# Barriers replaced by narrow waits, weight sums moved into the K/V phase, and PSUM emptying moved behind the next quantization, in an attention plus ternary FFN block on eight cores

## The chip, the cores and the metric

The kernel runs on all 8 NeuronCores of one Trainium2 chip. The cores do not exchange data: each computes 1024 of the 8192 rows of the output. The time is that of the slowest core, in device microseconds, as the median of several executions. The profile shows one execution on the slowest of its cores, here core 1.

## The reference, cut to what matters

```python
# x: (2, 4096, 2048). Weights: w_dq (1536,2048), w_uq (2048,1536), w_dkv (512,2048),
# w_ukv (4096,512), w_out (2048,2048), w_gate and w_up (8192,2048), w_down (2048,8192)
def weight_quant(w):                       # three values: -scale, 0, +scale
    scale = clip(mean(abs(w)), 1e-5)       # one mean over the whole matrix
    return clip(round(w / scale), -1, 1) * scale
def act_quant(x):                          # 8 bits, scale by the row's largest value
    s = 127 / clip(max(abs(x), axis=-1), 1e-5)
    return clip(round(x * s), -128, 127) / s
def bitlinear(x, w): return act_quant(x) @ weight_quant(w).T
def attn(x):                               # 16 heads of 128, causal
    q = x @ w_dq.T @ w_uq.T
    k, v = split(x @ w_dkv.T @ w_ukv.T)
    return softmax(q @ k.T / sqrt(128) + mask) @ v @ w_out.T
xn = layernorm(x)
y = x + attn(xn) + bitlinear(silu(bitlinear(xn, w_gate)) * bitlinear(xn, w_up), w_down)
```

The scales of the three large matrices need the sum of absolute values of each whole matrix before any of it can be quantized.

## The kernel before

The whole program is written out by one Python function, `emit`, once for each engine. Every wait is written by hand: `inc` counts an engine's own semaphore and waits for it, `wt(engine, semaphore, value)` waits, `dinc` counts a DMA by 16, and `barrier()` (L255) lets every engine wait for all others and for all DMAs so far. In the code T is TensorE (PE in the profile), V is VectorE (DVE), S is ScalarE (ACT), G is GpSimd (POOL), SY is SyncE (SP).

The stages of a core, with the times of core 1:

- P0a (0 to 744 us): layernorm of 4608 key rows in 36 tiles, transposes, and the 512-wide compressed keys and values `ckv`. P0b (to 920): the same for the core's 1024 own rows, with 8-bit quantization. P0c (to 1032): w_ukv loaded, the quantized rows transposed and stored.
- P0d (to 1165) and P0e (to 1340): the two query projections, weights streamed by `stream_blocks` (L509), 12 and 16 column blocks.
- Attention (to 3153): eight groups of two heads (loop at L670). In a group PE first makes K (18 banks of 128x512, L681, copied to `kg` by DVE, L687) and V (36 banks of 128x256, L693, copied to `vg`, L699) in four banks in turn, and then runs the sweep over 36 key tiles: scores (L602), exp on ACT (L609), row sums (L641), values (L645). The border between the core's two halves depends on the core, so the sweep stands in the program eight times, each under `If_eq` (L709), and a core skips seven of them: core c skips c before its own and 7 - c behind it.
- P1out (to 3325): output projection, L747, result to DRAM.
- P2a (3385 to 4660): gate and up for 16 chunks `hc` of 512 hidden columns. For a chunk, SP loads eight 1 MB blocks, DVE quantizes them (L833, L836 for gate into `tg`, L841, L844 for up into `tu`; two sets, by `hc % 2`), PE runs 128 gate matmuls into all eight banks (one bank for each row tile `tb`, L855), ACT applies silu into `hg` (L861), PE runs 128 up matmuls into the same banks (L871), and DVE multiplies each bank with `hg` into `hstg` (L880) and takes the maximum (L882); POOL stores `hstg` (L887). DVE's order is: quantize chunk hc, empty chunk hc, quantize chunk hc + 1. PE's first gate matmul of a chunk waits for all the emptying of the one before (`hv_prev`).
- P2b (to 4895): the hidden rows are read back (`hbuf`), quantized (L917 on ACT, L923 and L924 on DVE) and transposed (L932, L937), in four quarters for each of eight row tiles.
- P2c (to 5542): down projection, 16 output blocks `oc`. SP loads eight slabs of 512 KB in turn into two buffers, DVE quantizes them (L966, L968) into `tdq`, PE runs four quarters of 32 matmuls (L981) into one of two bank pairs, DVE copies the pair out (L987). DVE's order is: quantize oc, copy out oc, quantize oc + 1.
- P3: transposes back and the sum.

The sums of absolute values are made beside this by `pump_scale` (L373). It takes the next of 192 blocks of 1 MB, loads it (by POOL unless told otherwise) into one of one or two buffers, after the last sum on that buffer, and has it summed by ACT (`on_s=True`, L396) or DVE (L401). 36 blocks are summed on DVE in P0a; 8, 12 and 32 on ACT in P0c, P0d and P0e; 12 behind each of the eight sweeps on ACT (96); the last 8 on ACT behind P1out. Since PE's wait for the next group (`ms_sweeps`) is taken before them, the 12 sums run beside the K/V work of the next group. The calls behind a sweep are

```python
            ms_sweeps = cnt["mS"]
            for _ in range(6):
                pump_scale(1, (xt0,), on_s=True, dq=G, psem="p0")
                pump_scale(1, (xt1,), on_s=True, dq=SY, psem="c0")
```

Of the kernel before, what the change touches and what calls it, by code (L numbers as in the profile page):

```python
# [40 lines left out]
def build_nc():  # L41
# [184 lines left out]
    def emit(nc, ACTIVE, cnt):  # L226
# [443 lines left out]
        for g in range(NGRP):  # L670
# [3 lines left out]
            kv_ev = {}  # L674
            for kt in range(9):
                k0 = kt * 512
                for hh in range(HPG):
# [128 lines left out]
        hv_prev = 0  # L806
        for hc in range(FD):
# [5 lines left out]
            for q in range(4):  # L813
# [15 lines left out]
                if q == 0:  # L829
# [16 lines left out]
                    op0=ALU.is_gt, op1=ALU.subtract), V)  # L846
            tmg = [0] * NQT
            for q in range(4):
                wt(T, "mV", qg_q[q])
                if q == 0 and hc >= 1:  # L850
                    wt(T, "mV", hv_prev)
                for f4 in range(4):
                    fc = 4 * q + f4
# [22 lines left out]
            for tb in range(NQT):  # L876
                wt(V, "mT", tmu[tb])
                if hc >= 1 and tb == 0:
                    wt(V, "g2", hs_dg[hc - 1])
                inc(V.tensor_tensor(out=hstg[:, tb, :], in0=bank(tb), in1=hg[:, tb, :],  # L880
                                    op=ALU.mult), V)
                inc(V.reduce_max(out=hmaxa[:, hc, tb:tb + 1], in_=hstg[:, tb, :], axis=AX,  # L882
                                 apply_absolute_value=True), V)
            hv = cnt["mV"]
            hv_prev = hv
            wt(G, "mV", hv)
            gd = G.dma_start(out=hs_d.rearrange("(tb p) (hc c) -> tb p hc c", p=128, c=512)[:, :, hc, :].rearrange("tb p c -> p tb c"),  # L887
                             in_=hstg[:])
            hs_dg[hc] = dinc(gd, "g2")
# [242 lines left out]
```

How the kernel before makes its waits and increments, by code:

```python
        def then_inc(self, *a, **k):  # L196
            return self
# [1 line left out]
        def _wait_ge(self, *a, **k):  # L199
            return self
# [36 lines left out]
        def inc(instr, eng):  # L237
            s = e2s[id(eng)]
            cnt[s] += 1
            instr.then_inc(sems[s], 1)
            eng.wait_ge(sems[s], cnt[s])
            return cnt[s]
# [1 line left out]
        def dinc(instr, q):  # L244
            cnt[q] += 16
            instr.then_inc(sems[q], 16)
            return cnt[q]
# [1 line left out]
        def wt(eng, s, val):  # L249
            if val > 0:
                eng.wait_ge(sems[s], val)
# [3 lines left out]
        def barrier():  # L255
            for nm, _e in ENGS:
                cnt[nm] += 1
            me = EP.__getattribute__(
                {"tensor": T, "vector": V, "scalar": S, "gpsimd": G, "sync": SY}[ACTIVE],
                "_r") if False else None
            ap = {"tensor": T, "vector": V, "scalar": S, "gpsimd": G, "sync": SY}[ACTIVE]
            ap.nop().then_inc(sems["m" + {"tensor": "T", "vector": "V", "scalar": "S",
                                          "gpsimd": "G", "sync": "Y"}[ACTIVE]], 1)
            for nm, _e in ENGS:
                if nm != "m" + {"tensor": "T", "vector": "V", "scalar": "S",
                                "gpsimd": "G", "sync": "Y"}[ACTIVE]:
                    ap.wait_ge(sems[nm], cnt[nm])
            for dq in DMA_SEMS:
                if cnt[dq]:
                    ap.wait_ge(sems[dq], cnt[dq])
```

## Time and profile before

| | us |
|---|---|
| median of three runs | 5635.7 |
| lowest, highest | 5617.92, 5694.85 |
| the profiled execution | 5667.2 |
| its span on core 1, the slowest | 5665.4 |
| spans of cores 0, 2, 3 | 5649.4, 5622.2, 5647.3 |
| spans of cores 4, 5, 6, 7 | 5616.2, 5567.3, 5638.2, 5581.2 |

A row of the groups by line gives line, engine, operation, the tiles written and read, their shapes, the count, then busy time and mean of one, and last the idle time of that engine just before these instructions with what ended it. "issue" means that the profile shows nothing that the engine waited for. The chain of work that ended last is followed back from the end. Durations of matmuls are modelled: one takes about 0.38 us in the table even where the next starts 0.22 us behind it, so rates are read from start times.

### The profile page before, as it was taken

The numbers are of one execution on the slowest core, as the hardware profiler recorded it, in microseconds if no ns is written. First come the engines' busy times: TensorE is split into PE (matmuls) and PEld (weight loads), VectorE is DVE, ScalarE is ACT, GpSimd is POOL, SyncE is SP. The second block draws the span as 40 slices with busy tenths as digits, with TensorE's granted clock in tenths as the row PEclk, the third lists the DMA queues.
The fourth block names the chain that finished last, engine by engine and source line by source line (L and its number), as shares of the span: only waits on it lengthen the run. The fifth ranks groups of instructions, "written<-read, shape, count | busy, mean of one in ns | idle before, by whom it ended". The sixth has DMA issues, their size and how long they took to land.

```text
span 5665.4 us, 45000 instructions; the slowest of 8 cores (5567.3 to 5665.4 us)
## 1 busy us (share of the span) xinstructions
PE 3325.9 (59%) x13124; PEld 1231.6 (22%) x13124; DVE 2107.6 (37%) x2998; ACT 1099.9 (19%) x1101; POOL 129.8 (2%) x197
## 2 busy tenths in 40 slices
PE   2443422566565645645645447777787763588883
PEld 1111110222111111111111213333333321233332
DVE  3444434222122231221222124555445536644444
ACT  3333332222323223223233110000000002100000
POOL 0000000000000000000000000000000000000000
PEclk9655655788677776877778879988998885698775
DMA  4223213774012022021120554554344424333334
GB/s 145 104 104 119 97 52 104 210 235 127 31 61 91 1 91 71 21 92 32 60 91 17 159 176 127 149 148 119 119 134 149 149 95 149 109 109 112 97 104 148
DMA packets 344785, 610.04 MB, mean 108 GB/s; under 512 B 10530, under 2 KB 228130, under 8 KB 306978
## 3 DMA queue, kind: packets, MB, share of 16 engines
q1 hardware_dynamic: 310546, 399.08, 22.8%
q0 software_dynamic: 33808, 205.53, 11.3%
q8 instruction: 232, 3.80, 0.3%
q14 instruction: 199, 1.63, 0.1%
HBM read 554.24 MB, written 50.33 MB: 107 GB/s over the span
## 4 chain that ended last, share of the span: by engine, by line
PE 44%; DVE 20%; issue 14%; DMA 13%; ACT 8%; DVEq 1%; ACTq 0%; SPq 0%; POOL 0%; POOLq 0%; PEldq 0%
PE psp L981 7%; PE psp L602 4%; PE psb L871 4%; PE psb L641 3%; PE psp L871 3%; PE psb L645 3%; PE psp L693 3%; PE psp L681 3%; DMA xt<-wdT 2%; DVE tgq L836 2%; DMA gsq<-wgT 2%; ACT xntb L340 2%; DVE hstg L880 2%; DMA dslab<-wdT 2%; DMA pe<-wuT 2%
## 5 line engine op out<-in xcount | busy, mean ns | idle before, releaser
L981 PE MATMUL psp<-hqfm,tdq 128*128 128x512 bf16 x2048 | 528.0, 424 | 118.8 <-DVE tdq L968 108.1
L855 PE MATMUL psb<-tgq,xqfm 128*128 128x512 bf16 x1024 | 292.8, 399 | 238.3 <-DVE tgq L836 231.1
L609 ACT ACTIVATE ptile<-psp 128x1024 bf16<-128x1024 f32 x288 | 294.8, 1024 | 573.8 <-PE psp L602 572.0
L357 PE MATMUL psp<-identb,xntb 128*128 128x128 bf16 x352 | 93.3, 265 | 485.7 <-ACT xntb L340 286.1
L681 PE MATMUL psp<-ckv,wukv 128*128 128x512 bf16 x576 | 162.1, 407 | 331.4 <-issue 261.1
L981 PEld LDWEIGHTS psp<-hqfm,tdq 128*128 128x128 bf16 x2048 | 213.0, 106 | 433.4 <-issue 323.3
L629 DVE TENSOR_TENSOR ptile<-ptile,masksb 128x512 bf16<-128x512 bf16 x64 | 27.2, 425 | 738.8 <-ACT ptile L609 738.8
L855 PE MATMUL psp<-tgq,xqfm 128*128 128x512 bf16 x1024 | 287.7, 398 | 9.5
L871 PE MATMUL psb<-tuq,xqfm 128*128 128x512 bf16 x1024 | 272.9, 379 | 27.4 <-ACT hg L861 13.8
L602 PE MATMUL psp<-qfm,kg 128*128 128x512 bf16 x576 | 222.2, 475 | 109.9 <-PE psb L645 66.5
L871 PE MATMUL psp<-tuq,xqfm 128*128 128x512 bf16 x1024 | 270.7, 379 | 9.7
L641 PE MATMUL psb<-ptile,onesb 128*64 128x512 bf16 x576 | 215.3, 462 | 94.9 <-PE psp L602 66.7
L861 ACT ACTIVATE hg<-psb,sgs 128x512 f32<-128x512 f32 x64 | 44.0, 687 | 1130.6 <-PE psb L855 1123.5
L880 DVE TENSOR_TENSOR hstg<-psb,hg 128x512 f32<-128x512 f32 x64 | 44.3, 692 | 537.9 <-PE psb L871 528.8
L687 DVE CAST kg<-psp 128x512 bf16<-128x512 f32 x144 | 99.6, 692 | 387.9 <-PE psp L681 387.9
L396 ACT ACTIVATE xt<-xt 128x2048 f32<-128x2048 f32 x96 | 183.3, 1909 | 213.4 <-DMA xt<-wdT 122.7
L645 PE MATMUL psb<-ptile,vg 128*128 128x512 bf16 x576 | 217.9, 468 | 0.0
L693 PE MATMUL psp<-wukv,ckv 128*128 128x256 bf16 x1152 | 171.9, 271 | 74.7 <-PE psp L693 72.4
L855 PEld LDWEIGHTS psb<-tgq,xqfm 128*128 128x128 bf16 x1024 | 100.6, 101 | 386.2 <-issue 288.6
L968 DVE SCALAR_TENSOR_TENSOR tdq<-dslab,thr,dcma 128x1024 bf16<-128x1024 f32 x128 | 164.4, 1285 | 14.1 <-DVE dcma L966 0.9
L699 DVE CAST vg<-psp 128x256 bf16<-128x256 f32 x288 | 122.4, 425 | 122.1 <-PE psp L693 122.0
L362 DVE CAST xnf<-psp 128x128 bf16<-128x128 f32 x352 | 102.6, 292 | 174.8 <-PE psp L357 167.9
(157 smaller groups left out, 3963.8 us busy)
## 6 DMA issues: line engine op xcount, KB each, us to landing
gsq<-wgT SPq DMA_DIRECT2D x64, 1024.0 KB, 11.3
usq<-wuT SPq DMA_DIRECT2D x64, 1024.0 KB, 10.9
dslab<-wdT SPq DMA_DIRECT2D x128, 512.0 KB, 4.1
pa<-wgT POOLq DMA_DIRECT2D x36, 1024.0 KB, 5.0
xt<-xk SPq DMA_DIRECT2D x36, 1024.0 KB, 4.9
hs<-hstg POOLq DMA_DIRECT2D x16, 2048.0 KB, 12.0
hbuf<-hs SPq DMA_DIRECT2D x32, 1024.0 KB, 5.4
xt<-wdT POOLq DMA_DIRECT2D x28, 1024.0 KB, 5.8
```

The lines of the kernel that those rows point to most:

```text
L396: sm = inc(S.activation(out=sbuf[:], in_=sbuf[:], func=AF.Abs, accum_out=accTw[:, mi, col:col + 1]), S)
L602: mm = T.matmul(out=bank(sp + hh), lhsT=kg[:, hh, (j - jlo) * 128:(j - jlo + 1) * 128], rhs=qfm[:, h0 + hh, qc0:qc0 + 512], start=True, st ...
L609: a = S.activation(out=ptile[:, pb, :, :].rearrange("p h c -> p (h c)"), in_=bank2(sp), func=AF.Exp, scale=SCALE, bias=EXPB)
L641: T.matmul(out=(psb6 if hh == 0 else psb7)[0:64, :], lhsT=onesb[:, 0:64], rhs=ptile[:, pb, hh, :], start=st, stop=sp_)
L645: mm = T.matmul(out=bank(hh), lhsT=vg[:, j - jlo, hh * 128:(hh + 1) * 128], rhs=ptile[:, pb, hh, :], start=st, stop=sp_)
L681: mm = T.matmul(out=bank(b), lhsT=wukv[:, cc, (h0 + hh) * 128:(h0 + hh + 1) * 128], rhs=ckv[:, cc, k0:k0 + 512], start=(cc == 0), stop=(cc ...
L693: mm = T.matmul(out=bank(b)[:, 0:HPG * 128], lhsT=ckv[:, cc, jj * 128:(jj + 1) * 128], rhs=wukv[:, cc, 2048 + h0 * 128:2048 + (h0 + HPG) * ...
L855: mm = T.matmul(out=bank(tb), lhsT=xqfm[:, fc, tb * 128:(tb + 1) * 128], rhs=tg[:, fc, :], start=(fc == 0), stop=(fc == FD - 1))
L871: mm = T.matmul(out=bank(tb), lhsT=xqfm[:, fc, tb * 128:(tb + 1) * 128], rhs=tu[:, fc, :], start=(fc == 0), stop=(fc == FD - 1))
L880: inc(V.tensor_tensor(out=hstg[:, tb, :], in0=bank(tb), in1=hg[:, tb, :], op=ALU.mult), V)
L968: e_done[ei % 2] = inc(V.scalar_tensor_tensor(out=fq, in0=fl, scalar=thr[:, 4:5], in1=fa, op0=ALU.is_gt, op1=ALU.subtract), V)
L981: mm = T.matmul(out=bank(bp + nh), lhsT=tdq[:, hcc, :], rhs=hqfm[:, hcc, nh * 512:(nh + 1) * 512], start=(hcc == 0), stop=(hcc == 63))
```

## The change

- P0d, P0e and the first group: two barriers go. POOL waits for PE's last P0d matmul, and in front of the first group POOL, DVE and PE wait for the ends of P0e on ACT and DVE; the first four banks carry waits for their last copies.
- The sums behind the sweeps go. In the K/V phase of each group DVE calls `pump_scale(1)` after every fourth copy, up to the 52nd of 54: 13 sums in a group, on DVE, with buffers `xt0` and `xt1`, both loaded by POOL. With the 88 before, that is all 192. `pump_scale` also waits for the last sum that used the same semaphore.
- P2a: DVE quantizes chunk hc + 1 before it empties chunk hc, and PE's first matmul into a bank waits for the product (L880) of that bank only.
- P2a to P2b: the barrier and SP's wait for all stores go. SP waits for the last quantization and, quarter by quarter, for the store that it reads. `cmp_a` moves out of `hbuf`'s place.
- P2b to P2c: the barrier goes; SP and DVE wait for ACT's last instruction.
- P2c: DVE quantizes block oc + 1 before it copies out block oc; PE waits for the copy two blocks back by the bank pair.
- P2c to P3: the barrier goes; POOL and SP wait for PE, PE for DVE.

```diff
-    cmp_a = AT("cmp_a", [128, FD, 512], BF16, offset=SB0 + 168 * KB)
+    cmp_a = AT("cmp_a", [128, 4, 512], BF16, offset=SB0 + 200 * KB)
...
+                lastp = sc_done.get(ps)
+                if lastp and lastp != prev:
+                    wt(dq, lastp[0], lastp[1])
...
             pump_scale(1, (pd0,), on_s=True)
-        barrier()
+        wt(G, "mT", cnt["mT"])
...
             pump_scale(2, (pe0, pe1), on_s=True)
-        barrier()
+        p0e_T = cnt["mT"]
+        p0e_V = cnt["mV"]
+        p0e_S = cnt["mS"]
...
-            kv_ev = {}
+            if g == 0:
+                kv_ev = {2: ev_bank.get(2, 0), 3: ev_bank.get(3, 0),
+                         4: tb_ev[4], 5: tb_ev[5]}
+                wt(G, "mS", p0e_S)
+                wt(G, "mV", p0e_V)
+                wt(V, "mS", p0e_S)
+                wt(T, "mV", p0e_V)
+            else:
+                kv_ev = {}
+            evi = 0
...
                     kv_ev[b] = inc(ev, V)
+                    evi += 1
+                    if evi % 4 == 0:
+                        pump_scale(1)
...
                 kv_ev[b] = inc(ev, V)
+                evi += 1
+                if evi % 4 == 0 and evi <= 52:
+                    pump_scale(1)
...
             ms_sweeps = cnt["mS"]
-            for _ in range(6):
-                pump_scale(1, (xt0,), on_s=True, dq=G, psem="p0")
-                pump_scale(1, (xt1,), on_s=True, dq=SY, psem="c0")
...
+            if pend is not None:
+                ehc, etmu = pend
+                for tb in range(NQT):
+                    wt(V, "mT", etmu[tb])
+                    if ehc >= 1 and tb == 0:
+                        wt(V, "g2", hs_dg[ehc - 1])
+                    inc(V.tensor_tensor(out=hstg[:, tb, :], in0=bank(tb), in1=hg[:, tb, :],
+                                        op=ALU.mult), V)
+                    ev_tb[tb] = cnt["mV"]
+                    inc(V.reduce_max(out=hmaxa[:, ehc, tb:tb + 1], in_=hstg[:, tb, :], axis=AX,
+                                     apply_absolute_value=True), V)
+                wt(G, "mV", cnt["mV"])
...
-                if q == 0 and hc >= 1:
-                    wt(T, "mV", hv_prev)
...
+                        if fc == 0 and hc >= 1:
+                            wt(T, "mV", ev_tb[tb])
...
-        wt(SY, "g2", cnt["g2"])
-        barrier()
...
+        for vv in sorted(sq_done.values()):
+            wt(SY, "mV", vv)
...
+                if tb == 0:
+                    wt(SY, "g2", hs_dg[4 * qt + 3])
...
-        barrier()
+        p2b_V = cnt["mV"]
+        p2b_S = cnt["mS"]
...
+        wt(SY, "mS", p2b_S)
+        wt(V, "mS", p2b_S)
+        ev_bank[4] = p2b_V
...
+            if pend_c is not None:
+                eoc, ebp, etm = pend_c
+                wt(V, "mT", etm)
+                ev = V.tensor_copy(out=ffnb[:, eoc, :], in_=bank2(ebp))
+                ev_bank[ebp] = inc(ev, V)
...
-            tm = tmq_prev[3]
-            wt(V, "mT", tm)
-            ev = V.tensor_copy(out=ffnb[:, oc, :], in_=bank2(bp))
-            ev_bank[bp] = inc(ev, V)
-        barrier()
+            pend_c = (oc, bp, tmq_prev[3])
...
+        wt(G, "mT", cnt["mT"])
         ao_dd = dinc(G.dma_start(out=aofm[:], in_=aos_d.rearrange("f p c -> p f c")), "g2")
+        wt(SY, "mT", cnt["mT"])
         wt(T, "g2", ao_dd)
+        wt(T, "mV", cnt["mV"])
```

## Rows read from the trace of the kernel before

**Rows 1.** The page of core 1: busy times, and the chain by engine.
```profile
PE 3325.9 (59%) x13124; PEld 1231.6 (22%) x13124; DVE 2107.6 (37%) x2998; ACT 1099.9 (19%) x1101; POOL 129.8 (2%) x197
PE 44%; DVE 20%; issue 14%; DMA 13%; ACT 8%; DVEq 1%; ACTq 0%; SPq 0%; POOL 0%; POOLq 0%; PEldq 0%
```
**Rows 2.** Groups by line, forms apart; busy, mean ns | idle before, releasers.
```profile
L981 PE MATMUL psp<-hqfm,tdq 128*128 128x512 bf16 x2048 | 528.0, 424 | 118.8 <-DVE tdq L968 108.1 <-PE psp L981 10.2 <-DVE dcma L966 0.5
L855 PE MATMUL psb<-tgq,xqfm 128*128 128x512 bf16 x1024 | 292.8, 399 | 238.3 <-DVE tgq L836 231.1
L681 PE MATMUL psp<-ckv,wukv 128*128 128x512 bf16 x576 | 162.1, 407 | 331.4 <-issue 261.1 <-ACT xt L396 37.1 <-PE psp L681 29.8
```
**Rows 3.** Timeline of P2a: start, us, engine, line [idle before]; 15 such PE borders.
```profile
3610.30 0.69 DVE L880 TENSOR_TENSOR hstg<-psb,hg 128x512 f32<-128x512 f32 x1 [32.14 <-PE psb L871]
3611.95 0.69 DVE L880 TENSOR_TENSOR hstg<-psb,hg 128x512 f32<-128x512 f32 x1 [0.17 <-DVE hmaxa L882]
...
3623.61 1.29 DVE L833 TENSOR_SCALAR cmp_a<-gsq,thr 128x2048 bf16<-128x2048 f32 x1 [0.25 <-DVE hmaxa L882]
3625.00 2.35 DVE L836 SCALAR_TENSOR_TENSOR tgq<-gsq,thr,cmp_a 128x2048 bf16<-128x2048 f32 x1
...
3627.60 1.01 PE L855 MATMUL psb<-tgq,xqfm 128*128 128x512 bf16 x2 [13.80 <-DVE tgq L836]
```
**Rows 4.** Timeline of P2c, end of a pass and start of the next.
```profile
5005.42 7.07 PE L981 MATMUL psp<-hqfm,tdq 128*128 128x512 bf16 x32 [0.26 <-PE psp L981]
...
5018.77 9.30 PE L981 MATMUL psp<-hqfm,tdq 128*128 128x512 bf16 x32 [6.29 <-DVE tdq L968]
```
**Rows 5.** Timeline of K and V copies on DVE, second group.
```profile
1594.92 0.69 DVE L687 CAST kg<-psp 128x512 bf16<-128x512 f32 x1 [0.58 <-PE psp L681]
...
1600.88 0.42 DVE L699 CAST vg<-psp 128x256 bf16<-128x256 f32 x1 [0.43 <-PE psp L693]
```
**Rows 6.** Timeline of PE at three gaps: of core 1, of core 7, of core 4.
```profile
1339.41 1.01 PE L681 MATMUL psp<-ckv,wukv 128*128 128x512 bf16 x2 [22.66 <-issue]
...
1850.48 2.17 PE L602 MATMUL psp<-qfm,kg 128*128 128x512 bf16 x4 [33.98 <-issue]
...
1790.37 6.46 PE L681 MATMUL psp<-ckv,wukv 128*128 128x512 bf16 x16 [15.81 <-issue]
```
**Rows 7.** Groups by line again: the sums on DVE, ACT's table loads before the sweeps.
```profile
L401 DVE TENSOR_REDUCE accTw<-pa 128x1 f32<-128x2048 f32 x36 | 82.3, 2286 | 6.2 <-DVE xnf L362 4.6 <-DVE ckv L437 1.5
L609 ACT ACT_TABLE_LOAD x8 | 10.3, 1283 | 401.7 <-PE psp L602 401.7
```
**Rows 8.** DMA issues: queue, count, KB each, median us to landing.
```profile
xt<-wdT POOLq DMA_DIRECT2D x28, 1024.0 KB, 5.8
pe<-wgT POOLq DMA_DIRECT2D x8, 1024.0 KB, 9.3
aofm<-aos POOLq DMA_DIRECT2D x1, 4096.0 KB, 18.2
```
**Rows 9.** The chain in order of time (start, us): attention's end, P1out's, P2a's, P2b's.
```profile
3102.18 1.28 ACT L396
...
3328.32 15.74 DMA pt<-wdT
...
4646.81 12.06 DMA hs<-hstg
4660.57 9.34 DMA hbuf<-hs
...
4896.74 4.15 DMA dslab<-wdT
```
**Rows 10.** Windows of V, P2a, P2c: us, five engines' busy, granted clock, DMA, GB/s.
```profile
1364.00:1395.00 31.00, 21.49 (x144) 11.49 (x144) 15.75 (x37) 0.00 (x0) 0.00 (x0) 1.00 0.00 1
...
3950.00:4010.00 60.00, 54.44 (x239) 22.82 (x236) 23.34 (x17) 5.50 (x8) 0.00 (x0) 1.00 0.47 140
...
5211.00:5245.00 34.00, 31.54 (x119) 12.35 (x116) 11.45 (x12) 0.00 (x0) 0.00 (x0) 0.81 0.33 93
```

More of the change, by code:

```diff
@@ L397, in pump_scale @@
                                           accum_out=accTw[:, mi, col:col + 1]), S)
-                    sc_done[id(sbuf)] = ("mS", sm)
+                    sc_done[id(sbuf)] = sc_done[ps] = ("mS", sm)
                 else:
@@ L402, in pump_scale @@
                                           apply_absolute_value=True), V)
-                    sc_done[id(sbuf)] = ("mV", vm)
+                    sc_done[id(sbuf)] = sc_done[ps] = ("mV", vm)
         xn_sm = [0] * (NKC + NQT)
@@ L805, in emit @@
         silu_sm = [0] * NQT
-        hv_prev = 0
+        ev_tb = [0] * NQT
+        pend = None
         for hc in range(FD):
@@ L846, in emit @@
                     op0=ALU.is_gt, op1=ALU.subtract), V)
+            if pend is not None:
[10 more added lines that the diff above has]
+                wt(G, "mV", cnt["mV"])
+                gd = G.dma_start(out=hs_d.rearrange("(tb p) (hc c) -> tb p hc c", p=128, c=512)[:, :, ehc, :].rearrange("tb p c -> p tb c"),
+                                 in_=hstg[:])
+                hs_dg[ehc] = dinc(gd, "g2")
             tmg = [0] * NQT
@@ L875, in emit @@
             tq_used[setq] = cnt["mT"]
[L876 to L889, printed above, removed]
-        wt(SY, "g2", cnt["g2"])
-        barrier()
+            pend = (hc, list(tmu))
+        ehc, etmu = pend
+        for tb in range(NQT):
+            wt(V, "mT", etmu[tb])
+            if tb == 0:
+                wt(V, "g2", hs_dg[ehc - 1])
+            inc(V.tensor_tensor(out=hstg[:, tb, :], in0=bank(tb), in1=hg[:, tb, :],
+                                op=ALU.mult), V)
+            inc(V.reduce_max(out=hmaxa[:, ehc, tb:tb + 1], in_=hstg[:, tb, :], axis=AX,
+                             apply_absolute_value=True), V)
+        wt(G, "mV", cnt["mV"])
+        gd = G.dma_start(out=hs_d.rearrange("(tb p) (hc c) -> tb p hc c", p=128, c=512)[:, :, ehc, :].rearrange("tb p c -> p tb c"),
+                         in_=hstg[:])
+        hs_dg[ehc] = dinc(gd, "g2")
+        for b_ in (4, 5, 6, 7):
+            tb_ev[b_] = cnt["mV"]
         maybe_stop('P2a')
@@ L897, in emit @@
         QS = ("w0", "w1", "x0", "x1")
+        for vv in sorted(sq_done.values()):
+            wt(SY, "mV", vv)
         for tb in range(NQT):
             for qt in range(4):
+                if tb == 0:
+                    wt(SY, "g2", hs_dg[4 * qt + 3])
                 if tb >= 1:
@@ L944, in emit @@
                             scalar2=None, op0=ALU.mult), V)
-        barrier()
+        p2b_V = cnt["mV"]
+        p2b_S = cnt["mS"]
         maybe_stop('P2b')
         dsrc = wd_d.rearrange("(hc p) (oc c) -> hc p oc c", p=128, c=128)
+        wt(SY, "mS", p2b_S)
+        wt(V, "mS", p2b_S)
+        ev_bank[4] = p2b_V
         tmq_prev = [0, 0, 0, 0]
         e_done = {0: 0, 1: 0}
+        pend_c = None
         for oc in range(FD):
@@ L984, in emit @@
                 tmq_prev[qt] = inc(mm, T)
-            tm = tmq_prev[3]
-            wt(V, "mT", tm)
-            ev = V.tensor_copy(out=ffnb[:, oc, :], in_=bank2(bp))
-            ev_bank[bp] = inc(ev, V)
-        barrier()
+            pend_c = (oc, bp, tmq_prev[3])
+        eoc, ebp, etm = pend_c
+        wt(V, "mT", etm)
+        ev = V.tensor_copy(out=ffnb[:, eoc, :], in_=bank2(ebp))
+        ev_bank[ebp] = inc(ev, V)
         maybe_stop('P2c')
+        wt(G, "mT", cnt["mT"])
         ao_dd = dinc(G.dma_start(out=aofm[:], in_=aos_d.rearrange("f p c -> p f c")), "g2")
+        wt(SY, "mT", cnt["mT"])
         wt(T, "g2", ao_dd)
+        wt(T, "mV", cnt["mV"])
         y_ev = [0] * NQT
```

## The prediction

> **What bounds the kernel now.** I read five views in this order. First the page: engine busy times, then the chain of work that ended last [rows 1]. TensorE is busy in 59% of 5665.4 us, DVE in 37%. The chain is 44% PE, 20% DVE, 14% issue, 13% DMA: no engine is full, and the kernel is a row of stages with joins. Then the groups by line, for what ended PE's idle time [rows 2]. The large entries are 238.3 us before the gate matmuls (L855), nearly all ended by DVE's quantizing (L836), 118.8 us before the down matmuls (L981), ended by L968, and 331.4 us before the first K matmuls of the head groups (L681), "issue". Last the timeline and the chain at each join, and the windows for the clock.
>
> What the reader is to see. **Gate/up stage:** PE stops 13.80 us at a chunk border (the one before 3627.60; there are 15), because DVE empties eight banks first and only then quantizes the next weights [rows 3]. **Down stage:** PE ends a pass at 5012.5, DVE copies it out and quantizes two slabs, PE starts again at 5018.77 after 6.29 us and its first 32 matmuls take 9.30 us instead of 7.07. A pass is four quarters of 7.07 + 0.26 = 29.3 us and the border adds 6.03 + 2.23 = 8.3: 37.6 us [rows 4]. **Attention:** K and V of a head pair are made at 1.28 and 0.85 us a bank with DVE 0.69 and 0.42 us busy in each [rows 5], at clock 1.00 [rows 10]. The abs-sum of a weight block runs on ACT beside it, off the path. PE then idles about 39 us between sweep and next pair while it skips six branches.
>
> **The change part by part, on core 1 of the profiled run.** The sum is made against its own 5665.4 us.
>
> (a) P0d, P0e, attention lose two barriers. In P0e the abs-sum loads set the end: PE was idle 22.66 us before 1339.41 [rows 6], and the new DVE wait on ACT's last sum keeps that. P0e's first abs-sum loads start 2 us earlier and the first four K banks are already filled: -6. Bounds 0 and -14.
>
> (b) The abs-sums go to DVE inside K/V: 13 per group. Each is L401's 2.286 us [rows 7]. V phase: four copies at 0.42 plus 0.15 between plus the sum is 4.6 us against PE's 4 x 0.85 = 3.4; nine times +1.2 = 11. K phase: four copies and the sum 5.7 against 5.1; four times +0.6 = 2.4. With the waits of PE for a bank and of DVE for PE behind each sum (0.1 to 0.2) I take 15.3. DMA: each of two buffers is needed again two sums later, 9.4 us in the V phase and 11.4 in the K phase; the sum takes 2.3, the way to the issue 0.6, the landing 5.8 us at the median for such a load, 9.3 for the first ones of P0e beside other weights [rows 8]. I take 6.7, near the first because nothing else loads; it just fits: +16 per group, 8 x 16 = +128. Bounds: +122 (never waited for) and +216 (landing 9.3 us: a pair takes 12.5 us, in the V phase 5.7 more than PE's 6.8, 4.5 x 5.7 + 1.5 = +27 per group). What is queued behind a late landing is every following K/V copy, and PE with it after four banks.
>
> (c) No abs-sum loads while PE skips branches. Core 7 skips seven before its sweep with no loads beside it in 33.98 us, 4.9 each; core 1's six behind its sweep, with the loads running, are the 261.1 and 37.1 us of L681 in [rows 2] less the first 22.66: 39.4 at each of seven borders [rows 6]. At 5 us each six take 30: -9 x 7 = -63. Bounds: 0 (the difference is of the code, not the traffic) and -71. The Trainium skill (Runtime: NRT & Kernel Launch, Instruction fetch mechanics) says that a taken branch out of the fetched pages must get its target by DMA. By that rule the loads and the skips share the DMA engines and the sum keeps its -63; by a count of instructions alone it would be 0.
>
> (d) ACT keeps the Exp table: the 1.28 us load stands on the chain before each sweep, and now only before the first [rows 7]: 7 x 1.28 = -9.
>
> (e) Behind the last sweep ACT worked at its table and sums from 3102.18 [rows 9] to 3153, with the barrier behind them. PE ends the sweep about then, so its skips (30 us) end it now at 3133: -20. On core 6, which skips one branch, it is 51 - 7 = -44.
>
> (f) 8 x 13 = 104 sums instead of 96 leave none of the eight whose loads ran from 3328.32 on [rows 9], to 3379. The 6 MB for the next stage are loaded there anyway; 4 MB took 18.2 us [rows 8], so I take 24: -27. Bounds -33 (18.2) and -20.
>
> (g) P2a. DVE's chunk border order is turned: quantize next, then empty. Quantizing is 8 x (1.29 + 2.35 + 0.27) = 31 us, emptying 8 x 1.65 = 13 [rows 3]; 44 of about 70 us, so DVE is done about 20 us before PE. At the border PE's fc = 0 matmul of each bank now waits for that bank only. The first emptying starts 3.5 us before PE's last matmul ends (3610.30 against 3613.8), the eighth product ends 7 x 1.65 + 0.70 - 3.5 = 8.8 later; PE itself needs 1.7 for eight, so it loses 7.4 instead of 13.8: 15 x 6.4 = 96. Of the 231.1 us that ended on L836, the 24 beyond 15 x 13.8 lie inside the chunks and go too: -120. Bounds -144 (borders at 5.8 us) and -33 (all eight products and maxima needed, 13.2).
>
> (h) P2a to P2b. The 12.06 us store and 9.34 us load [rows 9] lie behind work: three of the four loads are early, and the first three quarters (32 of them in 4670 to 4895, 7.0 each) cover the fourth: -21 (bounds -9, the store still waited for, and -22). P2b to P2c: 4.15 us slab load [rows 9] and barrier: -7. SP's moved waits hold only loads that come later.
>
> (i) P2c. With the slabs of the next pass quantized in this one, PE has four quarters of 7.32 us, 29.3 instead of 37.6 [rows 4]. The 6.29 us stop holds a copy (about 1.2) and two slabs, so DVE needs some 2.4 a slab, 4.8 a quarter, and a slab buffer turns round in 4.15 [rows 9] + 2.4 = 6.5; both under 7.3. 15 x 8.3 = -124. P2c took 636 us from its first matmul, 43 more than 15 x 37.6 + 29.3: in its later part the clock read 0.81 [rows 10], a quarter then 7.07 / 0.81 = 8.7. A pass of 36 instead of 29.3 costs 6.5, so the stretch was 7 passes of 43, some 300 us; if it keeps its length it covers 8.5 shorter ones, 55: +12 to +15. Net -109. The last join: -2.
>
> Sum: -6 +128 -63 -9 -20 -27 -120 -21 -7 -109 -2 = -256, so 5409 on core 1. Core 6 (span 5638.2) has no such gap, so (c) is 0 and (e) -44: -217, 5421. It is the slowest then. The profiled execution was 5667.2 us, 31.5 above the median of three, so the forecast is 5423 - 31.5, rounded to 5395.
>
> **Rivals.**
> R1, late landings in (b): at 9.3 us 8 x 11 = +88, 5483. For it: two loads on POOL's one queue; against: nothing else loads then.
> R2, the skips stay as long: core 1 becomes 5472, 5442 at the median. Core 7's 33.98 speaks against it; for it, core 4 skipped three in 15.81 us with loads running, 5.3 each [rows 6].
> R3, a denser PE is granted less. In P2c it was 0.81 at PE 31.5 of 34 us busy [rows 10]. At 8.7 against 7.07 us per 32, all 4096 matmuls of P2a cost +209 and the rest of P2c +45: 5649, no change. Against: P2a held 1.00 with PE 54.4 of 60 us busy [rows 10]. The Trainium skill (TensorE: Matmul & The Clock Gate, Seeing it yourself) says that a die with three cores in dense matmuls goes to 13/16 clock and stays there while the load lasts; by that rule R3 would be the case, and this trace, where P2a is at 1.00 with eight cores at work, does not agree.
> R4, PE half idle in K/V falls to 1.2 GHz (0.50): K banks take 2.0 us, 18 x 0.55 x 8 = +80, 5475. Against: 1.00 in the V phase with PE 21.5 of 31 us busy [rows 10].
> R5, slower than before: the landings in (b) decide alone. Beyond 7 us each us costs some 6 us per group, 48 in all; the gain is 240 us, so at 12 us all is lost, and at 13 the time is about 5670. The longest of [rows 8] is 9.3.
> R6, the change doesn't reach the path: the new waits (DVE on ACT at P0e, DVE's emptying at the borders) stop as long as the barriers. P2a -33 instead of -120 gives 5482.
>
> **How the numbers follow.** Forecast 0.55 (own range 5340 to 5450); R1 0.11, R2 0.12, R3 0.08, R4 0.06, R5 0.03, R6 0.05. A change of 2% (5523 and 5748) is what a measurement can tell. Faster: all but R3 and R5, and 0.03 of misses within the others, 0.86. Same 0.11. Slower 0.03. Range 5320 to 5500: it takes in R1, R2, R4, R6 and leaves out R3, R5 and the forecast's tails, 0.2.
>
> **What would show it.** (b) K/V of a group 72 us instead of 56, DVE idle for "DMA xt" under 3 us a group. (c) L681's idle about 30 us on core 1. (d) one Exp table load. (g) borders of 7 to 8 us. (i) no gap between passes, 29.3 us each, or about 36 at 0.81. Wrong if K/V goes past 80 us, if P2a reads 0.81, or if the skips stay at 39.

## The result, and the profile after

Ten runs of each kernel: 5466.8 us median for the changed one (5422.4 to 5486.3), 5665.6 for the one before (5617.9 to 5694.9). The ratio is 0.964, with a 95% interval of 0.960 to 0.969: **faster, by 199 us**. The forecast was 5395 us, in a range of 5320 to 5500. It was tied to the first three runs of before, whose median was 5635.7; against that the forecast gain was 241 us. In some executions of any kernel one die is over 1% longer at a lower granted clock: medians here are of all executions, ratios, intervals and figures core by core of the others.

The profiled execution took 5486.2 us, 5484.7 on its slowest core, again core 1. First its page: busy times and the chain by engine.

```profile
PE 3483.7 (64%) x13124; PEld 1267.1 (23%) x13124; DVE 2345.4 (43%) x3102; ACT 882.8 (16%) x886; POOL 154.4 (3%) x245
PE 52%; DVE 19%; issue 15%; DMA 7%; ACT 6%; DVEq 1%; PEldq 1%; SPq 0%; ACTq 0%; POOL 0%; POOLq 0%
```

PE's share of the chain rose from 44 to 52% and DMA's fell from 13 to 7 [rows 1]. PE's busy time rose too, by 158 us, with the same 13124 matmuls: somewhere they run slower. The groups by line, forms apart, say where (busy, mean ns of one | idle before, releasers).

```profile
L1028 PE MATMUL psp<-hqfm,tdq 128*128 128x512 bf16 x2048 | 454.4, 380 | 25.2 <-PE psp L1028 17.4 <-DVE tdq L1010 6.8 <-DVE dcma L1008 0.8
L888 PE MATMUL psb<-tgq,xqfm 128*128 128x512 bf16 x1024 | 310.8, 421 | 53.3 <-DVE hstg L871 33.9 <-DVE tgq L854 8.1 <-PE psb L904 4.1
L710 PE MATMUL psp<-wukv,ckv 128*128 128x256 bf16 x1152 | 289.2, 404 | 102.2 <-PE psp L710 68.7 <-DVE kg L701 30.4 <-DVE vg L716 3.1
L695 PE MATMUL psp<-ckv,wukv 128*128 128x512 bf16 x576 | 163.2, 409 | 268.0 <-issue 207.1 <-DVE kg L701 32.5 <-PE psp L695 22.4
L404 DVE TENSOR_REDUCE accTw<-xt 128x1 f32<-128x2048 f32 x104 | 237.7, 2286 | 21.2 <-DVE vg L716 13.1 <-DVE kg L701 5.1 <-DMA xt<-wuT 2.5
L614 ACT ACT_TABLE_LOAD x8 | 10.3, 1283 | 945.9 <-PE psp L607 945.9
```

Against [rows 2]: the wait of the down matmuls (now L1028) fell from 118.8 to 25.2 us, of one half of the gate matmuls (L888) from 238.3 to 53.3, of the K matmuls (L695) from 331.4 to 268.0. But the V matmuls (L710) take 404 ns in the mean; before they took 271. The sums on DVE (L404) are 2286 ns each as forecast and waited 2.5 us in all for a landing. ACT still loads the Exp table eight times, not once.

The stages of core 1, from the first and last matmul of each line in the timelines, in us. "Low" is the 1.2 GHz level, granted clock 0.50.

| | before | after | change | forecast |
|---|---|---|---|---|
| start to the end of the first K/V | 1394.3 | 1407.6 | +13 | +10 |
| K/V of the seven other groups | 7 x 55.2 | 7 x 73.6 | +129 | +112 |
| from V to the first scores, 8 | 39.3 | 36.8 | -2 | 0 |
| sweeps with the table loads, 8 (time at low clock) | 875.5 (479) | 897.5 (541) | +22 | -9 |
| last scores to next K, 7 | 391.4 | 324.4 | -67 | -63 |
| last scores to output projection | 75.9 | 56.1 | -20 | -20 |
| output projection | 162.9 | 189.4 | +26 | 0 |
| to the gate/up stage | 64.5 | 34.6 | -30 | -27 |
| gate/up stage | 1245.3 | 1178.2 | -67 | -120 |
| to the down stage | 270.6 | 246.0 | -25 | -28 |
| down stage | 634.8 | 472.5 | -162 | -109 |
| to the end | 124.5 | 126.5 | +2 | -2 |
| sum | | | -181 | -256 |

The three large differences from the forecast in the last stages (output projection, gate/up and down stage) have one part in common: a stretch at granted clock 0.81. Windows of core 1 in the output projection, late gate/up and the whole down stage show it (us, busy times of five engines, clock, DMA):

```profile
3237.00:3427.00 190.00, 148.07 (x512) 55.19 (x512) 40.10 (x47) 0.00 (x0) 14.67 (x15) 0.78 0.38 102
4100.00:4240.00 140.00, 126.65 (x439) 48.05 (x437) 78.94 (x64) 5.50 (x8) 2.34 (x2) 0.75 0.42 137
4886.00:5358.00 472.00, 453.58 (x2047) 196.14 (x2046) 275.11 (x267) 0.00 (x0) 0.00 (x0) 1.00 0.50 140
```

The down stage, at 0.81 for 262 us before, now had 1.00 throughout; the output projection had 137 us at 0.81 (+26) and gate/up 265 us: four of its periods took 80.4 to 81.6 us, where others took 71.7. On core 4, which saw 0.81 in neither stage in either run, gate/up went from 1237.0 to 1141.5 (-96), the down stage from 592.3 to 472.5 (-120), the output projection stayed at 164. Those are the gains of the change in these stages.

### The profile page after: what moved, and what is told of

It reads as the page before. It is cut to its first block, busy times and chain, and to the rows that moved or that the text cites. A ratio compares the mean times of both kernels' runs of the same rounds, so it can differ in the third digit from the quotient of the medians.

```text
span 5484.7 us, 44659 instructions; the slowest of 8 cores (5351.4 to 5484.7 us)
## 1 busy us (share of the span) xinstructions
PE 3483.7 (64%) x13124; PEld 1267.1 (23%) x13124; DVE 2345.4 (43%) x3102; ACT 882.8 (16%) x886; POOL 154.4 (3%) x245
## 4 chain that ended last, share of the span: by engine, by line
PE 52%; DVE 19%; issue 15%; DMA 7%; ACT 6%; DVEq 1%; PEldq 1%; SPq 0%; ACTq 0%; POOL 0%; POOLq 0%
PE psp L1028 6%; PE psp L710 4%; PE psb L888 4%; PE psp L888 4%; PE psp L607 4%; PE psb L904 4%; PE psb L646 4%; PE psp L904 4%; PE psb L650 4%; DVE accTw L404 3%; ACT xntb L340 2%; DVE hqfm L974 2%; DMA pe<-wuT 2%; PE psb L435 2%; DMA dslab<-wdT 1%
## 5 line engine op out<-in xcount | busy, mean ns | idle before, releaser
L1028 PE MATMUL psp<-hqfm,tdq 128*128 128x512 bf16 x2048 | 454.4, 380 | 25.2 <-PE psp L1028 17.4
L710 PE MATMUL psp<-wukv,ckv 128*128 128x256 bf16 x1152 | 289.2, 404 | 102.2 <-PE psp L710 68.7
L888 PE MATMUL psp<-tgq,xqfm 128*128 128x512 bf16 x1024 | 314.2, 419 | 58.8 <-DVE hstg L871 49.2
L888 PE MATMUL psb<-tgq,xqfm 128*128 128x512 bf16 x1024 | 310.8, 421 | 53.3 <-DVE hstg L871 33.9
L695 PE MATMUL psp<-ckv,wukv 128*128 128x512 bf16 x576 | 163.2, 409 | 268.0 <-issue 207.1
L904 PE MATMUL psb<-tuq,xqfm 128*128 128x512 bf16 x1024 | 286.2, 394 | 25.2 <-ACT hg L894 13.9
L904 PE MATMUL psp<-tuq,xqfm 128*128 128x512 bf16 x1024 | 284.2, 394 | 10.5 <-ACT hg L894 0.9
L1028 PEld LDWEIGHTS psp<-hqfm,tdq 128*128 128x128 bf16 x2048 | 196.3, 98 | 283.0 <-issue 57.5
L404 DVE TENSOR_REDUCE accTw<-xt 128x1 f32<-128x2048 f32 x104 | 237.7, 2286 | 21.2 <-DVE vg L716 13.1
L710 PEld LDWEIGHTS psp<-wukv,ckv 128*128 128x128 bf16 x1152 | 123.8, 125 | 267.7 <-issue 231.4
L1008 DVE TENSOR_SCALAR dcma<-dslab,thr 128x1024 bf16<-128x1024 f32 x128 | 96.4, 753 | 158.5 <-PE psp L1028 104.6
```

Source lines behind the costliest of these rows:

```text
L695: mm = T.matmul(out=bank(b), lhsT=wukv[:, cc, (h0 + hh) * 128:(h0 + hh + 1) * 128], rhs=ckv[:, cc, k0:k0 + 512], start=(cc == 0), stop=(cc ...
L710: mm = T.matmul(out=bank(b)[:, 0:HPG * 128], lhsT=ckv[:, cc, jj * 128:(jj + 1) * 128], rhs=wukv[:, cc, 2048 + h0 * 128:2048 + (h0 + HPG) * ...
L1028: mm = T.matmul(out=bank(bp + nh), lhsT=tdq[:, hcc, :], rhs=hqfm[:, hcc, nh * 512:(nh + 1) * 512], start=(hcc == 0), stop=(hcc == 63))
```

## Experiments

Twelve kernels ran. Stage times below are of core 1 of the profiled execution, unless another core is named.

### e1 and e2: the change in two halves

```diff
+            for _ in range(6):
+                pump_scale(1, (xt0,), on_s=True, dq=G, psem="p0")
+                pump_scale(1, (xt1,), on_s=True, dq=SY, psem="c0")
```

e1 is the changed kernel with the sums taken out of K/V and put back behind the sweeps as above. e2 is the kernel before with the attention part alone.

> The changed kernel with its 96 sums put back behind the sweeps on ACT, two DMA queues, the rest of the change kept. On core 1 the two profiles give for the attention part: first K banks -28 us, K/V of the first group +41, of the seven others +18.4 each, gaps between last scores and next K -9.6 each (55.9 to 46.3), end of the last sweep to the output projection -20, output projection to gate/up -30: together +20. Theory A (the sums in K/V cost more than the shorter skips give back): K/V 55 us, gaps 56, and about 20 us faster than the changed kernel, some 220 under the kernel before. Theory B (the attention part is a gain, and what looks like its cost is the scatter of the clock): 20 us slower than the changed kernel, 180 under the kernel before.

> The kernel before with the attention part of the change alone (two early barriers, sums on DVE in K/V); gate/up and down stages and their barriers as before. Theory A: +20 us against the kernel before, no difference that counts. Theory B: 20 us or more faster. Prediction on record: its terms for this part come to +3. K/V of a group 73 us, gap 46 on core 1.

e1: 5421.5 us median of four (5376.6 to 5458.1), no interval; the kernel before beside it 5650.0. e2: 5694.6, ratio 1.0063, interval 1.0024 to 1.0103. In e1 K/V is back to 55.5 us and the gap to 54.5; gate/up 1137, down 473. In e2 K/V is 73.3, the gap 45.2; gate/up 1238, down 594. Four executions are too few to tell 20 us; e11 is e1 again, beside the changed kernel itself (e12).

> The changed kernel with the sums back behind the sweeps, beside the changed kernel on the same chip, to tell 20 to 30 us. Theory A: 5420 to 5450 us, 20 to 40 under the changed kernel. Theory B: not under it.

> The changed kernel itself, for the comparison with the sums behind the sweeps: 5450 to 5490 us, ratio 0.964 to the kernel before by every theory.

e11: 5373.4, ratio to the kernel before beside both 0.9538 (0.9481 to 0.9595). e12: 5444.4, ratio 0.9659 (0.9613 to 0.9704). **Theory A holds, B falls:** alone, the attention part makes the kernel slower by 0.2 to 1.0%, and the changed kernel with the sums back behind the sweeps is faster by 71 us. The whole gain is in the two feed-forward stages and their joins. The 71 are more than the 20 to 40 expected, and a part of that is which core counts. Core by core (medians of six each) e12 is longer by 39, 60, 41, 91, 81, 80, 70 and 101 us on cores 0 to 7: little where many branches are skipped behind the sweep, most on core 7, which skips none there. On core 1, from which the expectation came, it is 60 and not 20 to 40; the rest is open. On core 4, the slowest of e12, three skip there: K/V costs the same 129 us (7 x 73.6 against 7 x 55.2), the gaps give back 26 (7 x 31.2 against 7 x 34.9). The same holds in e2: core 7 is 112 us longer than in the kernel before, core 2, the slowest there, only 15, and the time is that of the slowest core. So e2's 0.6% understates what the sums in K/V cost.

### e3 and e4: the same sums on ACT, held back or free

```diff
                     if evi % 4 == 0:
-                        pump_scale(1)
+                        wt(S, "mV", kv_ev[b])
+                        pump_scale(1, on_s=True)
```

This is e3, in both loops; e4 has the second added line without the wait.

> The changed kernel with the 13 sums of a group on ACT, each started by the same K/V copy behind which DVE's stood; loads on POOL's queue as before. Theory A (DVE's 2.29 us sums in a row with the copies are the whole price): K/V back to 55 us from 73, PE at clock 1.00 in it, gaps stay at 46 on core 1, 147 us less than the changed kernel less up to 5 us a group where ACT ends late: 100 to 147 us faster than it. Theory C (the loads beside K/V slow its copies or matmuls): K/V stays above 65. Theory D (the low clock of PE in the V phase is set by something other than its stalls): V phase stays at 45 us at clock 0.50.

> The same 13 sums on ACT with no wait for a copy: ACT starts them when the sweep ends, so that their loads run while PE skips branches, as in the kernel before. Theory A1 (the loads lengthen the skips): gap on core 1 back from 46 to 56, K/V 55, so 7 x 10 = 70 us slower than the gated version on core 1, nothing on core 7, which skips nothing behind its sweep. Theory A2 (the skips became shorter by the code between them): gap stays at 46 and this kernel is as fast as the gated one.

e3: 5355.9 us, ratio 0.945 (0.930 to 0.960, from three executions, classed as unclear). It is 294 us under its kernel before, where the changed one is 199 under: 95 more, near the 100 to 147 of Theory A. e4: 5378.7 us, no interval. The V phase of the fourth group as a window, of the changed kernel and then of e3:

```profile
2071.00:2116.00 45.00, 35.84 (x143) 15.48 (x144) 34.69 (x44) 0.00 (x0) 4.33 (x9) 0.50 0.61 202
```
```profile
2015.00:2045.00 30.00, 20.89 (x140) 11.19 (x140) 15.17 (x36) 14.28 (x16) 4.23 (x8) 1.00 0.70 242
```

45 us at clock 0.50 against 30 at 1.00, with more traffic beside it in e3 (242 against 202 GB/s). So theories C and D fall: the loads don't hold K/V up, nor is the clock low without DVE's sums; DVE's sums do both. K/V of all groups of e3 is 24.9 + 30.4 us. ACT ends its last sums late, by some 2 us a group: core 1 stands 51 us in front of its eight sweeps instead of 37.

The gap is the test of the skips. PE's rows for the first K matmuls of a group, three of e3 and then three of e4:

```profile
1990.79 4.84 PE L695 MATMUL psp<-ckv,wukv 128*128 128x512 bf16 x12 [28.86 <-issue]
2209.61 5.83 PE L695 MATMUL psp<-ckv,wukv 128*128 128x512 bf16 x16 [28.27 <-issue]
2428.35 7.07 PE L695 MATMUL psp<-ckv,wukv 128*128 128x512 bf16 x16 [28.24 <-issue]
```
```profile
1998.89 1.44 PE L695 MATMUL psp<-ckv,wukv 128*128 128x512 bf16 x3 [36.62 <-issue]
2220.53 1.86 PE L695 MATMUL psp<-ckv,wukv 128*128 128x512 bf16 x4 [38.49 <-issue]
2450.54 5.81 PE L695 MATMUL psp<-ckv,wukv 128*128 128x512 bf16 x16 [34.72 <-issue]
```

The two programs differ by 13 waits of ACT in a group. With the loads held back six skips take 28.5 us in these rows, with the loads running 36.6; over all seven gaps the means are 28.3 and 38.0. Means of the whole gap: 45.0 against 54.7 on core 1; on core 7, which skips nothing behind its sweep, 18.2 against 18.1. **The loads lengthen the skips (A1)**, as step (c) had it. ACT's sums run there too in e4; they were not separated from their loads. But the DMA queues of one such gap point at the loads. First e3 (1961 to 1991 us), then e4 (1961 to 1999): queue and kind, packets, MB, share of 16 engines.

```profile
q8 instruction: 11, 0.18, 3.9%
```
```profile
q0 software_dynamic: 1034, 7.55, 56.4%
q8 instruction: 11, 0.18, 2.4%
```

In each of the seven gaps of either run the same 11 instruction packets of 16 KB land on q8, about two for each skipped branch; in e4 they come further apart, beside 7.55 MB of loads. The Trainium skill (Runtime: NRT & Kernel Launch, Instruction fetch mechanics) says that a taken branch's target is fetched by DMA when it lies outside the fetched pages; these two runs agree, at 4.7 us a skip without and 6.3 with the loads.

### e5, e9 and e10: why the clock is low in the V phase

```diff
-                b = 2 + (jj % 4)
+                b = 2 + ((jj + 2) % 4)
```

This is e5. e9 cuts each sum in two, `sbuf[:, 0:D // 2]` and `sbuf[:, D // 2:D]`, one behind every second copy. e10 is both.

> The changed kernel, only the order of banks in the V phase turned by two, so that the first V bank is the one copied longest ago and PE doesn't stand 3.6 us behind the copies of the last two K banks. Theory E (that stop lets the clock fall, and at 1.2 GHz a V bank takes 1.27 us, so PE bounds the V phase): clock 1.00 in the V phase, which goes from 45.0 to the 41 us that DVE needs (9 x 4.6), K/V from 73.4 to about 66. Theory F (the clock falls because PE has a third of idle time as long as DVE sets the pace): clock still 0.50, V phase 45, K/V about 70 to 73.

> The changed kernel with each sum of 128x2048 cut into two of 128x1024 and one placed after every second copy; the first half is overwritten by the second, so the scales leave half of each block out. DVE's work in the V phase is nearly the same (4 copies and two halves, about 4.8 us for four banks), its longest stop of the copies falls from 2.3 to 1.2 us. Theory J (long stops of PE pull the clock down in the V phase): clock 1.00 there, V phase about 43 us. Theory F (any pace of DVE that leaves PE a share of idle time does, however it is cut): clock 0.50, V phase 45 to 47 us.

> The kernel with halved sums and, in addition, the V banks turned by two (half of each block is left out of the scales again). Each of the two edits alone left a stop of PE at the K to V step, 2.1 us with turned banks and 3.7 to 4.1 us with halved sums, and in both the clock fell at that stop. Here DVE's pace is the same and the longest stop is about 1 us. Theory K (a stop at the step lets the clock fall, and then PE at 1.2 GHz is kept low by its own slow pace): clock 1.00 through most of the V phase, which takes the 42 to 43 us that DVE needs. Theory F (DVE's pace alone lets it fall): 0.50 within the first quarter of the phase, V phase 44 to 46 us.

The V phases as windows, e5 and then e9:

```profile
2023.00:2069.00 46.00, 35.23 (x144) 15.20 (x142) 37.90 (x46) 0.00 (x0) 4.75 (x9) 0.53 0.60 209
```
```profile
2078.00:2122.00 44.00, 34.88 (x140) 14.86 (x139) 35.69 (x53) 0.00 (x0) 4.76 (x9) 0.50 0.55 192
```

The clock stayed low in all three; K/V took 71, 73 and 72 us. But none took the stop away as meant. It moved two banks on (e5, 1.90 us idle), stayed in front of V (e9, 4.00) or moved and shrank to 1.7 us in most groups (e10), and on core 1 the clock fell around that stop each time, 2 us behind it at the latest. So E, J and K are not refuted by these. What speaks for F is the rare case of a clock that came back within the phase. PE in e9, last group of core 1, some banks of it:

```profile
3005.67 1.01 PE L743 MATMUL psp<-wukv,ckv 128*128 128x256 bf16 x4 [0.26 <-PE psp L743]
3006.94 0.60 PE L743 MATMUL psp<-wukv,ckv 128*128 128x256 bf16 x4 [0.26 <-PE psp L743]
...
3012.47 0.60 PE L743 MATMUL psp<-wukv,ckv 128*128 128x256 bf16 x4 [0.64 <-DVE vg L749]
...
3015.05 0.60 PE L743 MATMUL psp<-wukv,ckv 128*128 128x256 bf16 x4 [1.13 <-DVE vg L749]
```

Banks come 1.27 us apart up to 3006.94 and 0.85 apart behind it: clock 1.00. PE then waits for DVE, never longer than 1.13 us, and at 3016.8 the clock is 0.50 again. e10 shows the same in one group of core 1 (1.00 from 2314.8 to 2325.0), and in e6, with whole sums, the clock came back in the sixth group and fell again behind stops of 1.34 and 2.06 us. So waits of about 1 us, as DVE's pace makes them, are enough for a fall; in the other groups the stop at the step may be what starts it.

At 0.50 a V bank takes PE 1.27 us, 36 of them 45.7. What DVE needs is seen in its rows: two sums of the changed kernel, then two of e5, both at clock 0.50.

```profile
2079.13 2.29 DVE L404 TENSOR_REDUCE accTw<-xt 128x1 f32<-128x2048 f32 x1 [0.17 <-DVE vg L716]
2084.19 2.29 DVE L404 TENSOR_REDUCE accTw<-xt 128x1 f32<-128x2048 f32 x1 [0.17 <-DVE vg L716]
```
```profile
2037.99 2.29 DVE L404 TENSOR_REDUCE accTw<-xt 128x1 f32<-128x2048 f32 x1 [0.17 <-DVE vg L716]
2042.84 2.29 DVE L404 TENSOR_REDUCE accTw<-xt 128x1 f32<-128x2048 f32 x1 [0.17 <-DVE vg L716]
```

In the changed kernel a sum comes every 5.07 us, four banks of PE, and DVE waits some 0.25 us in each round: PE is just the bound. In e5 PE keeps its lead through the phase, DVE hardly waits, and its own round is 4.84 us (four copies and a sum, 0.17 us between each), not the 4.6 of the prediction and of e5's expectation. Nine rounds are 43.6 us, so the low clock costs about 2 of the 18 us a group and DVE's sums the rest. This also makes the four theories hard to tell by time: whole sums or halves, DVE needs 43 to 46 us in a V phase at either clock. The times of e5 (5472), e9 (5568 and 5442) and e10 (5414) are not compared.

### e6 and e7: what PE loses at a chunk border

```diff
                     ev_tb[tb] = cnt["mV"]
+                for tb in range(NQT):
                     inc(V.reduce_max(out=hmaxa[:, ehc, tb:tb + 1], in_=hstg[:, tb, :], axis=AX,
```

This is e6, products first. e7 waits for `ev_tb[NQT - 1]` at every bank.

> The changed kernel, only DVE's order at the chunk border changed: eight products first, then eight maxima. Theory G (PE's loss at a border is the row of DVE instructions up to the last product, now 8 x 1.65 less the lead): a product costs 0.8 us, the last ends about 3 us behind PE's last matmul, of which PE works 1.7: 1 to 2 us lost instead of 7.0 in the first gate matmuls, period 71.6 to about 66, gate/up stage 1139 to about 1060 us. Theory H (the loss is something else, such as the start of the gate matmuls on new weights): period stays 71.6.

> The changed kernel, only that PE's first gate matmul waits for the product of the last bank. Prediction on record: border loss 8.8 us and the way to PE instead of 7.4, since PE's own 1.7 us for eight matmuls no longer lie beside the products. Theory G: 1.5 to 2 us more per border, stage 1139 to about 1165 us. Rival R6 of the prediction (the emptying at the border stops PE as long as the old order): 13 us per border, 1240.

The first gate matmuls of a chunk in the timeline of the changed kernel (full clock before them), with DVE's first product of that border in front:

```profile
3810.82 0.69 DVE L871 TENSOR_TENSOR hstg<-psb,hg 128x512 f32<-128x512 f32 x1 [27.07 <-PE psb L904]
```
```profile
3814.68 0.59 PE L888 MATMUL psb<-tgq,xqfm 128*128 128x512 bf16 x2 [0.36 <-PE psb L904]
3815.11 0.38 PE L888 MATMUL psp<-tgq,xqfm 128*128 128x512 bf16 x1
3816.62 0.38 PE L888 MATMUL psp<-tgq,xqfm 128*128 128x512 bf16 x1 [1.13 <-DVE hstg L871]
3818.27 0.59 PE L888 MATMUL psp<-tgq,xqfm 128*128 128x512 bf16 x1 [1.28 <-DVE hstg L871]
3819.93 0.59 PE L888 MATMUL psp<-tgq,xqfm 128*128 128x512 bf16 x1 [1.07 <-DVE hstg L871]
3821.58 0.59 PE L888 MATMUL psb<-tgq,xqfm 128*128 128x512 bf16 x1 [1.07 <-DVE hstg L871]
3823.23 1.44 PE L888 MATMUL psb<-tgq,xqfm 128*128 128x512 bf16 x3 [1.07 <-DVE hstg L871]
3824.47 1.91 PE L888 MATMUL psp<-tgq,xqfm 128*128 128x512 bf16 x4
```

Each bank waits for its product, 1.65 us apart, and the matmuls lengthen from 0.38 to 0.59 us: the clock has gone to 0.50. On core 4 the 11 or 12 matmuls behind the waits start 0.43 us apart, not 0.22. The same place in e6, and its DVE:

```profile
3699.06 0.59 PE L889 MATMUL psb<-tgq,xqfm 128*128 128x512 bf16 x2 [0.36 <-PE psb L905]
3699.49 1.25 PE L889 MATMUL psp<-tgq,xqfm 128*128 128x512 bf16 x4
3701.23 0.38 PE L889 MATMUL psb<-tgq,xqfm 128*128 128x512 bf16 x1 [0.49 <-DVE hstg L871]
3702.09 0.81 PE L889 MATMUL psb<-tgq,xqfm 128*128 128x512 bf16 x3 [0.49 <-DVE hstg L871]
3702.74 1.03 PE L889 MATMUL psp<-tgq,xqfm 128*128 128x512 bf16 x4
```
```profile
3701.26 0.69 DVE L871 TENSOR_TENSOR hstg<-psb,hg 128x512 f32<-128x512 f32 x1 [0.17 <-DVE hstg L871]
3702.05 6.21 DVE L875 TENSOR_REDUCE hmaxa<-hstg 128x1 f32<-128x512 f32 x8
```

PE stops for 1 us in all and four matmuls take 1.03 us, not 1.91: clock 1.00. The period falls from 71.6 to 63.4 us, the stage from 1139 (cores without 0.81) to 1017, more than the 80 expected: of 8.2 us per border 5.8 are the waits, 2.4 the low clock behind them (11.5 matmuls by 0.21), which the expectation had left out. Theory G holds. e6 took 5291.2 us in its one execution. e7: the stage takes 1149 us, 10 more than the changed kernel where 25 were expected and R6 said 1240. One wait of 8.91 us stands in place of the short ones. Waiting bank by bank is worth 0.7 us a border; the turned order is worth the rest.

### e8: what the experiments point to

e8 has the sums on ACT, held back only until the first K copy of a group (`if evi == 1: wt(S, "mV", kv_ev[b])`), and e6's products first.

> The changed kernel with the sums on ACT, held back only until the first K copy of the group (loads stay out of the skips, ACT isn't late at the sweep), and with the products first. By the profiles: K/V 55 instead of 73 us, gap 45 on core 1, the 14 us that the version with every sum held lost before its sweeps gone, gate/up stage 80 us shorter. From the 5356 of that version 14 + 80 less: about 5262, ratio to the kernel before 0.931. If Theory G is wrong 5342, 0.945. If the loads don't fit beside K/V when they start with it (6.5 pairs of about 8.1 us are 53 of 55 us), ACT is late again: 5276.

5172.9 us, ratio 0.916 (0.912 to 0.920): 475 us under the kernel before, where the changed one was 199 and 204 us under. K/V 55.3, gap 47.0, gate/up 1017, and 43 us in front of the sweeps instead of e3's 51. No core of it was at 0.81. It beats the 5262 expected by 89 us; 42 of them are gate/up, which gained 122 instead of 80, the rest is not assigned.

## Why the prediction was right, and where it was not

**(a), first group.** The wait of DVE on ACT's last sum kept P0e's gap, as forecast: PE's first K banks start at 1311.35 and then stand 20.80 us. The two rows show who is late.

```profile
1336.17 0.69 DVE L701 CAST kg<-psp 128x512 bf16<-128x512 f32 x1 [25.07 <-ACT pe L399]
1337.01 1.87 PE L695 MATMUL psp<-ckv,wukv 128*128 128x512 bf16 x4 [20.80 <-DVE kg L701]
```

**(b), K/V.** Forecast 72 us a group, measured 73.6, and the mechanism was the forecast one, DVE's 2.29 us in a row with the copies. The landings fitted (5.2 us), so R1 and R5 did not come. R4 came in the half that the forecast did not price: it feared 0.50 in the K phase, but the K phase went to 1.00 after its first banks as before (28.6 us), and it was the V phase that fell. It costs about 2 us there, not R4's 10. The term that was mis-sized is DVE's round in the V phase, 4.84 us and not 4.6, nine times a group. The stop of 3.6 us behind the last K sum is in the K phase's 28.6. The argument against R4, 1.00 in the V phase of before [rows 10], held only for PE at its own pace of 0.85 us a bank [rows 5].

**(c), skips.** Forecast -9 a group, measured -9.6, and e3 against e4 shows that loads and sums beside the skips are the cause. R2 falls. **(e), (f)** -20 and -30 against -20 and -27.

**(d), Exp table.** Wrong. All eight loads are still there; I took ACT's switch back from the sums as their only reason, and none stands between the sweeps now. Why they stay is open. The load also didn't get shorter or move: in both traces it starts 1.1 us behind a sweep's first scores and ends just before the first exp, so nothing of the 9 us was gained.

**(g), gate/up.** The border was right: on core 4 the period fell from 78.2 to 71.6 us, 6.6 a border where 6.4 was forecast, though 2.4 of what is still lost are the clock, which the forecast did not see. The failed step is "the 24 beyond 15 x 13.8 lie inside the chunks and go too": core 4 gained 96, just the borders. Of these 24, 7.8 us stood in front of the stage's very first matmul, where there is no border, and 8.1 stand there now. On core 1, 265 us at 0.81 took back 38 (1178 against 1140) of the 105 left without it.

**(h)** -25 against -28. **(i), down stage.** No gap between passes, as forecast:

```profile
4998.14 7.07 PE L1028 MATMUL psp<-hqfm,tdq 128*128 128x512 bf16 x32 [0.26 <-PE psp L1028]
5005.60 7.07 PE L1028 MATMUL psp<-hqfm,tdq 128*128 128x512 bf16 x32 [0.40 <-PE psp L1028]
5012.93 7.07 PE L1028 MATMUL psp<-hqfm,tdq 128*128 128x512 bf16 x32 [0.26 <-DVE ffnb L1018]
```

A pass starts at 5005.60; before, PE stood 6.29 us there [rows 4]. Sixteen passes took 472.5 us, 29.5 each; core 4 gained 120 (forecast 124 without the clock's part). The step that failed on core 1 is that the stretch at 0.81 would stay in this stage and cost 12 to 15: it was elsewhere. What the down stage got back (42) the output projection and gate/up lost (26 and 38). That these nearly cancel is luck, and the forecast lost little by it as a sum, but it named the wrong core: not core 6 but core 1, where these stretches fell on it and its sweeps stood 62 us longer at low clock (+22).

**The rivals.** R3 (denser stages are granted less) falls: core 4 had gate/up and down denser at 1.00, and nine of the twelve experiments, most of them with the dense stages, show no 0.81 on any core in the execution traced. R6 falls (e7). The 42 us between the forecast gain of 241 and the measured 199 are of one sign with (g)'s 24, (b)'s 17 and (d)'s 7; that they are just these is worked out from one execution and not shown. The time alone would not tell the forecast from its rivals: 5467 lies nearer to R4's 5475, R1's 5483 and R6's 5482 than to 5395, and it is the stage times and e3, e4 and e7 that rule on them. (The prediction's own 5423 - 31.5 is 5391.5, put at 5395.)

The forecast was carried by the joins of the feed-forward stages, and there the order of DVE's work, more than the barriers, was the cause: for gate/up e6 and e7 show it, for the down stage it is read from the rows and no run separated it. The part of the change that looked like an exchange (shorter skips for longer K/V) was a loss, as its own terms had nearly said: they came to +3.

## What to carry to other kernels

Move bookkeeping to the engine that is idle in that phase, not to the one that empties PSUM: the same 13 sums cost 18 us a group on DVE, and on ACT nothing in K/V and 1 to 2 us in front of the sweep. In a join, let what frees the waiting engine go first and all that only needs SBUF (here the maxima) after it. And look where loads run: beside a busy PE they are free, beside skipped branches each skip costs 1.6 us more. Where only the slowest core counts, look at every core before calling a change free.

## What the runs showed of the hardware

- **The clock fell behind short stops and stayed down at a slow pace.** V banks issued every 0.85 us kept 1.00 for the whole phase (30.6 us). Where DVE holds PE back by stops of 1 to 4 us it fell to 0.50, a bank took 1.27 us, and the clock stayed down for nearly the whole phase (45 of 45 us) with no wait longer than 0.43 us in it. Short waits of 1.1 to 1.3 us before matmuls at a chunk border did the same for the 11 matmuls behind them. How far stop and pace share in it stays open.
- **A skipped branch costs PE an instruction fetch.** 4.7 us each without other DMA, 6.3 with 1 MB loads beside it, with about two instruction packets of 16 KB a branch (e3, e4).
- **0.81 comes in stretches, on pairs of cores, whatever the stage.** Before: cores 0 and 1 from 5201 on, 6 and 7 from 5127, 2 and 3 from 1053, 4 and 5 from 1084, each over 327 to 345 us. After: cores 0 and 1 at 3255 to 3416 and 3979 to 4304, cores 2 and 3 at 349 to 510 and from 1073, the other four never. In nine of the twelve experiments (all but e4, e5, e7) there was none at all in the execution traced. The Trainium skill (TensorE: Matmul & The Clock Gate, Seeing it yourself) has the whole die fall to this level with three dense cores and stay while the load lasts; these traces don't agree: two cores of a die fall, also in the sparse first stage, and come back in the middle of a dense one. What sets it stays open.
